# A recommendation tower with held tables: tables and ids laid side by side in memory, fewer and larger loads, and the weights' low halves computed one unit later

## The reference

```python
e = jnp.stack([tbl_0[ids[:, 0]], ..., tbl_25[ids[:, 25]]], axis=1)      # (2048, 26, 128)
combined = jnp.concatenate([e, r_dense_x[:, None, :]], axis=1)          # (2048, 27, 128)
z = jnp.einsum('bfd,bgd->bfg', combined, combined)[:, TRIU_I, TRIU_J]   # (2048, 351)
h = jnp.concatenate([z, r_dense_x], axis=1)
h = jnp.maximum(h @ W_top1 + b_top1, 0.0)      # W_top1 (479, 512)
h = jnp.maximum(h @ W_top2 + b_top2, 0.0)      # W_top2 (512, 256)
y = h @ W_top3                                 # W_top3 (256, 1)
```

## Time and profile before

| | before |
|---|---|
| median of 3 runs | 418.01 (416.83 to 420.61) |
| the profiled execution's own time | 419.08 |
| its span, first to last instruction | 417.0 |
| mean granted TensorE clock in the span | 0.935 |
| busy: PE, PEld, DVE, ACT, POOL | 341.8, 324.6, 248.9, 203.5, 253.0 |
| moved by DMA | 44.80 MB, mean 107 GB/s |

### The profile page before, as it was taken

How to read it: one execution, slowest core, us unless ns; L and a number is a source line. 1 busy time by engine, 2 the same in 40 slices (tenths; PEclk the granted TensorE clock), 3 DMA queues, 4 the chain that set the end, 5 groups by cost and what they waited for, 6 DMA issues and landing times.

```text
span 417.0 us, 9831 instructions
## 1 busy us (share of the span) xinstructions
PE 341.8 (82%) x4178; PEld 324.6 (78%) x4178; DVE 248.9 (60%) x298; ACT 203.5 (49%) x273; POOL 253.0 (61%) x262
## 2 busy tenths in 40 slices
PE   0567679699995999699986999499994999599837
PEld 0566569598995989698986989399994989599736
DVE  3699488744675548754776558564585448662113
ACT  0565584346651385337553474336661475335612
POOL 4788877777777777777777577753777277000000
PEclk9999999889996999999996999889996999979959
DMA  6999525562446325762538225660446315500120
GB/s 175 249 243 255 139 71 149 121 127 52 129 108 132 92 60 150 128 124 53 143 94 138 73 67 149 113 125 23 114 119 123 81 47 146 68 5 2 38 75 0
DMA packets 38237, 44.80 MB, mean 107 GB/s; under 512 B 19561, under 2 KB 31473, under 8 KB 38194
## 3 DMA queue, kind: packets, MB, share of 16 engines
q1 hardware_dynamic: 28602, 24.32, 27.7%
q0 software_dynamic: 8192, 16.79, 16.5%
q10 hardware_dynamic: 1400, 3.07, 2.5%
HBM read 37.95 MB, written 6.20 MB: 106 GB/s over the span
## 4 chain that ended last, share of the span: by engine, by line
PE 50%; DVE 16%; DMA 13%; SPq 7%; issue 7%; ACT 4%; ACTq 3%; DVEq 0%
DVE hot L653 13%; PE ps_gram L434 13%; PE ps_mix L452 11%; PE ps_feat L416 7%; DMA ids_row<-in_ids_t 7%; PE ps_feat L417 7%; DMA products_dram<-gram 6%; SPq L302 6%; PE ps_feat L402 5%; PE ps_mix L485 3%; ACTq L289 2%; SPq L296 2%; PE ps_mix L490 1%; PE ps_feat L452 1%; ACT feat L564 1%
## 5 line engine op out<-in xcount | busy, mean ns | idle before, releaser
L378 POOL DMA_INDIRECT emb<-in_tbl,idx x256 | 252.4, 986 | 100.2 <-issue 76.2
L653 DVE TENSOR_TENSOR hot<-ids_row,ps_rows 125x1024 fp32r<-125x1024 int32 x160 | 186.6, 1215 | 59.6 <-DMA ids_row<-in_ids_t 30.4
L416 PE MATMUL ps_feat<-hot,held_h 125*128 125x256 f32 x640 | 166.4, 297 | 23.9 <-DVE held_l L639 20.1
L564 ACT COPY feat<-ps_feat 128x512 f32<-128x512 f32 x104 | 125.8, 1214 | 76.7 <-PE ps_feat L402 42.8
L417 PE MATMUL ps_feat<-hot,held_l 125*128 125x256 f32 x640 | 161.2, 289 | 0.0
L416 PEld LDWEIGHTS ps_feat<-hot,held_h 125*128 125x128 f32 x640 | 126.8, 198 | 25.9 <-issue 15.2
L417 PEld LDWEIGHTS ps_feat<-hot,held_l 125*128 125x128 f32 x640 | 126.5, 198 | 0.0
L434 PEld LDWEIGHTS ps_gram<-feat 128*54 128x54 f32 x2048 | 54.7, 130 | 11.2 <-ACT feat L564 5.7
L434 PE MATMUL ps_gram<-feat 128*54 128x54 f32 x2048 | 59.8, 215 | 2.5 <-ACT feat L564 2.3
L452 PE MATMUL ps_mix<-z_h,w1z_h 117*128 117x256 f32 x87 | 28.5, 327 | 34.6 <-DVE z_l L695 34.6
L585 ACT ACTIVATE h_h<-ps_mix,b_sb 128x256 fp32r<-128x256 f32 x29 | 13.8, 475 | 86.9 <-DVE h_x L701 86.9
(11 more groups left out here) (77 smaller groups left out, 248.3 us busy)
## 6 DMA issues: line engine op xcount, KB each, us to landing
ids_row<-in_ids_t SPq DMA_DIRECT2D x80, 128.0 KB, 7.1
products_dram<-gram SPq DMA_DIRECT2D x30, 189.0 KB
emb<-in_tbl,idx POOLq DMA_INDIRECT x256
z_raw<-products_dram SPq DMA_DIRECT2D x93, 26.0 KB
held_raw<-in_tbl ACTq DMA_DIRECT2D x5, 448.0 KB
held_raw<-in_tbl SPq DMA_DIRECT2D x5, 448.0 KB
dense<-in_dense_t SPq DMA_DIRECT2D x8, 128.0 KB
w1z_raw<-in_W_top SPq DMA_DIRECT2D x3, 234.0 KB
```

The source lines that it names most:

```text
L378: pool.indirect_dma_start(emb[:, h, f, :], None, table, bass.IndirectOffsetOnAxis(ap=idx[:, i * UNIT + h, f:f + 1].bitcast(u32), axis=0),) ...
L416: nc.tensor.matmul(dst, held_h[:, o, c, :], hot[:, n % 2, c, :], start=c == 0, stop=False)
L564: nc.scalar.copy(feat_v[:, f, b], src).then_inc(act_out, 1)
L653: nc.vector.tensor_tensor(hot[:, n % 2, chunks, :], bass.AP(ids_row, (n % SLOTS) * UC, [[SLOTS * UC, HR], [0, PC], [1, UC]]), row_nums[:, ...
```

## The change

- **Ids.** The ids of the held tables are laid out by unit in one array `ids_h`, one unit's ten tables side by side. One transfer now brings the ids of two tables (`PER_ROW = 2`). There are ten slots, so five transfers a unit, each into its own place; each waits only until the one-hots of the same two tables of the unit before have been made. SP issues all five ahead of the products' store.
- **Held tables.** They are padded to 1024 rows and laid side by side in one array `held` of 128 partitions, so a table is one transfer. ACT issues the ids of the gathers and tables 0 and 1; SP issues the other eight between the id transfers. ACT makes a copy of one element ahead of its first cast. In unit 0 ACT casts three tables ahead, and DVE takes a table's low half before its one-hot, not behind.
- **Weights.** `weights_low` moves from unit 0's product part to unit 1's table part, one behind each one-hot of tables 2 to 7. PE waits for all six at its first l1 step and no longer between units 0 and 1.
- **Smaller.** `store_y` is issued ahead of `products_through_dram`. `h2` shares memory with `z_h`, `y` with `h1_x`, with a wait of ACT and one of DVE for that. The matrix products and one-hots are 128 partitions high and no longer 125.

```diff
-    SLOTS = 7
+    SLOTS = NH
+    PER_ROW = 2
+    AHEAD = 2
...
         def load_table(eng, o):
-            rows_of = held[o][1].rearrange("(p c) d -> p c d", p=HR)
-            for p, end in ((0, EVEN), (EVEN, HR)):
-                eng.dma_start(held_raw[p:end, o, :, :], rows_of[p:end, :, :]).then_inc(held_in[o], 16)
+            eng.dma_start(held_raw[:, o, :, :], held[:, o * HC * D:(o + 1) * HC * D].rearrange("p (c d) -> p c d", c=HC)
+                          ).then_inc(held_in[o], 16)
...
-            def load_ids_row(i, o):
-                n = i * NH + o
-                reached(sp, hot_made, (n - SLOTS + 1) * PIECES)
...
+            def load_ids_rows(i, p):
+                reached(sp, hot_made, ((i - 1) * NH + (p + 1) * PER_ROW) * PIECES)
+                sp.dma_start(ids_row[:, p * PER_ROW:(p + 1) * PER_ROW, :].rearrange("q o b -> q (o b)"),
+                             ids_h[i:i + 1, p * PER_ROW * UC:(p + 1) * PER_ROW * UC].to_broadcast([128, PER_ROW * UC])
+                             ).then_inc(ids_row_in[p], 16)
...
-            sp.dma_start(idx[:], ids_g[:, :, :]).then_inc(ids_in, 16)
-            for o in range(SLOTS):
-                load_ids_row(0, o)
+            load_ids_rows(0, 0)
+            for o in range(AHEAD, NH):
+                if o % PER_ROW == 0:
+                    load_ids_rows(0, o // PER_ROW)
+                load_table(sp, o)
             load_dense(0)
-            for o in range(NH // 2, NH):
-                load_table(sp, o)
-            for o in range(SLOTS, NH):
-                load_ids_row(0, o)
             for i in range(UNITS):
                 if i == 0:
                     weights()
                 if not is_last(i):
-                    for o in range(SLOTS):
-                        load_ids_row(i + 1, o)
+                    for p in range(NH // PER_ROW):
+                        load_ids_rows(i + 1, p)
                     load_dense(i + 1)
-                products_through_dram(i)
-                if not is_last(i):
-                    for o in range(SLOTS, NH):
-                        load_ids_row(i + 1, o)
                 if i > 0:
                     store_y(i - 1)
+                products_through_dram(i)
...
                     if k == 0:
                         pe.wait_ge(dense_low, j + 1)
+                        pe.wait_ge(w_split, NW)
...
-            for o in range(NH // 2):
+            act.dma_start(idx[:], ids_g[:, :, :]).then_inc(ids_in, 16)
+            for o in range(AHEAD):
                 load_table(act, o)
-            for o in range(2):
+            act.wait_ge(cleared, 2)
+            nc.scalar.copy(h1_x[:, 1, 0:1], ones[:])
+            for o in range(3):
                 table_high(o)
...
                     if kind == "hot":
+                        if i == 0 and k[1] == 0:
+                            table_low(k[0])
                         one_hot(i, *k)
-                        if i == 0 and k[1] == PIECES - 1:
-                            table_low(k[0])
+                        if i == 1 and k[1] == PIECES - 1 and k[0] - 2 < NW:
+                            weights_low(k[0] - 2)
...
-                        if i == 0 and k < NW // 2:
-                            weights_low(2 * k)
-                            weights_low(2 * k + 1)
```

More of the change, by code:

```diff
@@ L27, in pairs, with dlrm_tower_kernel @@
     return out
-def dlrm_tower_kernel(nc, x_t, ids_g, ids_t, gathered, held, w1, b1, w2, b2, w3, out):
+def dlrm_tower_kernel(nc, x_t, ids_g, ids_h, gathered, held, w1, b1, w2, b2, w3, out):
     fp32 = mybir.dt.float32
@@ L38, in dlrm_tower_kernel @@
     UC = x_t.shape[1]
-    B, D = ids_t.shape[1], held[0][1].shape[1]
-    NG, NH = len(gathered), len(held)
+    UNITS, NH = ids_h.shape[0], ids_h.shape[1] // UC
+    D = gathered[0].shape[1]
+    B = UNITS * UC
+    NG = len(gathered)
     F = NG + 1 + NH
@@ L44, in dlrm_tower_kernel @@
     UNIT = UC // TILE
-    UNITS = B // UC
     S = 4
@@ L63, in dlrm_tower_kernel @@
     N1, N2 = H1 // 128, H2 // 128
-    ROWS = held[0][1].shape[0]
-    HC = -(-ROWS // 128)
-    HR = ROWS // HC
-    EVEN = HR // 16 * 16
+    HR = held.shape[0]
+    HC = held.shape[1] // (NH * D)
     PIECES = 2
     PC = HC // PIECES
-    SLOTS = 7
+    SLOTS = NH
+    PER_ROW = 2
+    AHEAD = 2
     BANKS = [(f, min(4, NG - f)) for f in range(0, NG, 4)]
@@ L77, in dlrm_tower_kernel @@
     assert UNIT == 2 and N1 == 4 and N2 == 2 and NH % 2 == 0
-    assert ZC * ZR == PAIRS and HC * HR == ROWS and PC * PIECES == HC and GB * M <= BANK
+    assert ZC * ZR == PAIRS and HR == 128 and PC * PIECES == HC and NH % PER_ROW == 0 and GB * M <= BANK
     def merged(*spans):
@@ L140, in dlrm_tower_kernel @@
         h1_x = sb("h1_x", [128, 2, UC], fp32)
-        h2 = sb("h2", [128, N2, UC], fp32)
+        h2 = nc.alloc_sbuf_tensor_at("h2", [128, N2, UC], fp32, offset=placed_at["z_h"])
+        y = nc.alloc_sbuf_tensor_at("y", [1, UC], fp32, offset=placed_at["h1_x"])
         def raw_and_low(name, shape, raw_shape=None, raw_name=None):
@@ L193, in dlrm_tower_kernel @@
         rows_in = [[sem(f"rows_in{h}_{w}") for w in range(NB)] for h in range(UNIT)]
-        ids_row_in = [sem(f"ids_row_in{p}") for p in range(SLOTS)]
+        ids_row_in = [sem(f"ids_row_in{p}") for p in range(NH // PER_ROW)]
         dense_in = sem("dense_in")
@@ L376, in gather @@
                         for f in range(first, first + count):
-                            table = gathered[f][1]
+                            table = gathered[f]
                             pool.indirect_dma_start(
@@ L543, in table_high @@
             def table_high(o):
-                act.wait_ge(held_in[o], 32)
+                act.wait_ge(held_in[o], 16)
                 nc.scalar.copy(held_h[:, o, :, :], held_raw[:, o, :, :]).then_inc(held_high, 1)
@@ L581, in later @@
                     reached(act, l1_done, j * N1)
+                    reached(act, weighed, j)
                     nc.scalar.copy(z_h[:, k, :], z_raw[:, k, :]).then_inc(z_high, 1)
@@ L607, in unit @@
                         later(i - 1, kind, k)
-                    elif kind == "hot" and k[1] == 0 and i == 0:
-                        table_high(k[0])
-            for o in range(NH // 2):
+                    elif kind == "hot" and k[1] == 0 and i == 0 and k[0] + 1 < NH:
+                        table_high(k[0] + 1)
+            act.dma_start(idx[:], ids_g[:, :, :]).then_inc(ids_in, 16)
+            for o in range(AHEAD):
                 load_table(act, o)
-            for o in range(2):
+            act.wait_ge(cleared, 2)
+            nc.scalar.copy(h1_x[:, 1, 0:1], ones[:])
+            for o in range(3):
                 table_high(o)
@@ L698, in later @@
                     dve.wait_ge(l1_done, j * N1 + k + 1)
+                    if k == 0:
+                        reached(dve, y_out, 16 * j)
                     if k >= 2:
@@ L779 @@
     lay["W_top1"] = lay["W_top1"][order]
-    lay["ids_t"] = lay["ids"].T
+    lay["ids_h"] = lay["ids"][:, held].reshape(-1, SAMPLES, HELD).transpose(0, 2, 1).reshape(-1, HELD * SAMPLES)
+    short = -fewest % 128
+    lay["held"] = _np.concatenate([_np.pad(lay.pop(f"tbl_{t}"), ((0, short), (0, 0))).reshape(128, -1) for t in held], 1)
     lay["ids"] = lay["ids"][:, gathered].reshape(-1, 128, len(gathered)).transpose(1, 0, 2)
@@ L792 @@
         ap[name] = nc.dram_tensor(f"in_{name}", a.shape, _mybir.dt.from_np(a.dtype), kind="ExternalInput").ap()
-    rows = lay["ids_t"].shape[1]
+    rows = lay["ids_h"].shape[0] * SAMPLES
     out = nc.dram_tensor("out_y", (1, rows), _mybir.dt.float32, kind="ExternalOutput").ap()
-    dlrm_tower_kernel(nc, ap["dense_t"], ap["ids"], ap["ids_t"], [(t, ap[f"tbl_{t}"]) for t in gathered],
-                      [(t, ap[f"tbl_{t}"]) for t in held], ap["W_top1"], ap["b_top1"], ap["W_top2"],
+    dlrm_tower_kernel(nc, ap["dense_t"], ap["ids"], ap["ids_h"], [ap[f"tbl_{t}"] for t in gathered],
+                      ap["held"], ap["W_top1"], ap["b_top1"], ap["W_top2"],
                       ap["b_top2"], ap["W_top3"], out)
```

10 lines of the change are left out of this document (1 added, 9 removed).

## The result

| | before | after |
|---|---|---|
| median | 418.75 (4 runs, 416.83 to 420.61) | 381.69 (4 runs, 378.92 to 382.68) |
| the profiled execution's span | 417.0 | 379.9 |
| mean granted TensorE clock | 0.935 | 0.978 |
| busy: PE, DVE, ACT, POOL | 341.8, 248.9, 203.5, 253.0 | 333.2, 247.8, 203.5, 252.2 |

The ratio of the times is 0.9105, with a 95% interval of 0.9039 to 0.917. The changed kernel is 37 faster. No engine has much less work: the time was waiting, and matrix work at a low clock.

What follows compares the result with a forecast made beforehand. Late ids held up DVE's one-hots and `z_l`, so PE waited and its clock fell. Terms -1.4 + 3.6 - 3.0 - 23.8 - 11.3 = -35.9, from the median 418.01: 382.1; range 375 to 395, the forecast's own 378 to 387.

Steps and rivals of the forecast that it cites:

- What bounds: Every unit: DVE's one-hots wait for table 7's late ids, so `z_l` is late and PE waits, then runs slowly.
- Ids, units 2 to 7: -23.8: DVE's one-hots in units 2 to 7 no longer wait for ids, as these come ahead of the products: -23.8.
- Clock: -11.3: Units 2 to 7, first z product to l1 chunk 1: PE's clock stays at its upper level, -11.3.
- the rival that it falls all the same: PE's clock behind z falls despite the shorter gap: +11.3, so 393.4; chance 0.16.
- Unit 1: +0.6: Unit 1: weights' low halves among DVE's one-hots cost 3.6, the ids' wait saves 3.0; together +0.6.
- I leave unit 1 its low clock: Unit 1: PE's gap before z stays long, so no clock gain is counted; if the clock stays up, another -2.5.
- The +3.6 and the -3.0: Unit 1: six weights' low halves on DVE add 3.6; the wait for ids that goes saves 3.0.
- Unit 0: -1.4: Unit 0: ACT copies rows 7 earlier, 57.31 to about 55.9, -1.4; bounds 0 and -4.
- at the same time as before: Unit 0: the gathers start when their ids are there, no later than before, and decide the product part's end.
- ACT's lateness: Unit 0: ACT copied rows 7 at 57.31, though PE was done at 55.80; casts of weights lay ahead.
- The gathers: Units 1 to 7: POOL's gathers don't bind, 16 to spare; rival that they bind late units, 388, chance 0.08.
- The low halves and POOL: Unit 1: six weights' low halves cost POOL at most 2.7, hidden in a margin of 9 less 1.7; term 0.

Runs made afterwards that it cites:

- e1: Kernel before with ten id slots, all ids issued ahead of the products' store, and the shared memory of `h2` and `y`; transfers keep 128 KB: 386.19, ratio 0.9202.
- The filler: Kernel before with 28 extra matrix products on PE ahead of its wait for z in units 1 to 7: 405.55, ratio 0.9673.
- e5: Changed kernel with the six low halves of the weights back in unit 0's product part: 376.27, ratio 0.8971.
- e9: Changed kernel with one extra one-hot on DVE, a delay, ahead of table 7's in each of units 2 to 7: 395.77, ratio 0.9437.
- e7: Changed kernel with the gathers' ids in two transfers, unit 0's on ACT's queue, the rest on SP's behind the tables: 380.39, ratio 0.9075.
- e10: Changed kernel with two extra one-hots on DVE, as delays, ahead of table 7's in each of units 2 to 7: 408.72, ratio 0.9747.
- e14: Kernel before with only the ids laid out by unit; seven slots, 128 KB transfers and three late ones as before: 411.52, ratio 0.9834.
- e12: As e1, but the ids come from an array of the ten held tables alone, in long rows by table: 385.81, ratio 0.9192.
- e11: As e1, but the ids come from an array with a unit's ten rows side by side: 377.62, ratio 0.8990.
- e4: Kernel before with the changed kernel's start and `ids_h`; weights' low halves stay in unit 0, ids in seven slots behind the products: 412.65, ratio 0.9823.

## Why the prediction was right, and where it was not

The two large terms and what decides them were right. That the total came within 0.4 of the measured median is luck in part: on the spans the sum of the terms was 1.2 short of the 37.1 measured, with unit 1 better than forecast by 2.6, units 2 to 7 by 0.8, and unit 0 worse by 2.25.

**What bounds.** Right. With the ids ahead of the products and, but for the shared memory, nothing else (e1), units 1 to 7 fall to 41.4 each.

**Ids, units 2 to 7: -23.8.** Right. The units lost 35.9, of which the stretches took 11.5 (next point); the rest is 24.4. PE's six gaps ahead of z shrank by as much, from 30.5 to 6.1.

**Clock: -11.3.** Right: the six stretches fell from 38.63 - 6.03 = 32.60 to 21.09, that is -11.5. I gave the rival that it falls all the same 0.16. The filler and the delays show what decides: PE's gap. But the margin is thinner than I thought. The gap is 1.02, and at 2.27 the clock falls in every unit.

**Unit 1: +0.6, measured -2.0.** The step that failed is the sentence "I leave unit 1 its low clock". The +3.6 and the -3.0 were right, as e5 confirms; the clock stayed up. I had put PE's gap there at 1.1 and up to 1.2 more, and it came out as that, at 2.34:

```profile
82.48 0.35 PE L446 MATMUL ps_mix<-den_h,w1d_h 128*128 128x256 f32 x1 [2.34 <-DVE w_l L642]
```

Behind this same gap of 2.34 the clock stayed up in the changed kernel and in e9, and fell in e7 and e10. So the size of the term, -2.5, was right and given as the other bound; which way it goes here is near chance, as far as one traced execution of each can tell.

**Unit 0: -1.4, measured +0.85.** The +0.85 is less than unit 0 differs by between executions, so whether it became longer is open. But two steps of the term failed. The gathers did not start "at the same time as before": their ids landed later on ACT's queue, and the first gather ran at 6.71 and not at 5.00. The first gather before and after:

```profile
5.00 1.09 POOL L378 DMA_INDIRECT emb<-in_tbl,idx  x1 [3.54 <-DMA idx<-in_ids]
```

```profile
6.71 1.09 POOL L372 DMA_INDIRECT emb<-in_tbl,idx  x1 [5.25 <-DMA idx<-in_ids]
```

In the runs whose whole ids of the gathers are on SP's queue it ran at 4.63 to 5.11, in those that have them on ACT's at 5.47 to 7.01. The second step matters more. The timeline of PE in unit 0, for the earlier trace rows:

```profile
50.68 0.63 PE L396 MATMUL ps_feat<-ident,emb 128*128 128x128 f32 x4 [1.78 <-DMA emb<-in_tbl,idx]
51.24 1.01 PE L428 MATMUL ps_gram<-feat 128*54 128x54 f32 x32
55.34 1.09 PE L396 MATMUL ps_feat<-ident,emb 128*128 128x128 f32 x4 [3.09 <-DMA emb<-in_tbl,idx]
56.36 6.46 PE L428 MATMUL ps_gram<-feat 128*54 128x54 f32 x160
```

```profile
56.36:62.82 6.46, 6.46 (x162) 6.40 (x161) 2.88 (x3) 3.80 (x6) 4.86 (x6) 0.62 0.27 74
```

ACT's lateness did go: it copied rows 7 at 56.46 and not at 57.31. But the table part ended 3.5 earlier, while the 32nd gather, at 52.69 (52.44 before), did not come earlier. PE now waited 1.78 and 3.09 for gathers, and the clock fell to 0.62 in the mean behind that. I applied the rule "a long wait of PE lowers the clock" to the place where the wait went, and not to the place where a new wait came. The two waits, and the low clock behind the second, are in every traced run with the new start. Where the clock stayed up in unit 0 (e14), the last 128 inner products took 3.44 and it ended at 59.13.

**The gathers.** That they don't bind units 1 to 7 was right, with either layout of the ids: all waits for them are in unit 0, and with the old layout the later units are as short (e1: 41.35 and 248.46). What the prediction has no term for is the layout. It took the new one as no more than a means to make one transfer of two. With the ids ahead and the old layout, unit 0 ends 7 later (70.41 and 70.15 against 63.24), with a gather 9.2 late in e1, and 8 to 9 of the gain are gone in the medians (e1 and e12 against e11). The sum came out because the change has both parts. The larger transfers did not show a gain: 80 transfers of 128 KB on the old start (377.62) stand beside 40 of 256 KB on the new one with the low halves in the same place (376.27). The Trainium skill (DMA: Bandwidth & Descriptors, Rules for kernel authors) advises to coalesce many small transfers into one. The run by unit against the one by table (3.4 and 10.1 to landing, at the same size and number) shows that here the place of the rows counted for more.

**The low halves and POOL.** The six in unit 1 cost POOL nothing that PE felt, as forecast; PE had no wait for gathers there.

## What to carry to other kernels

A short wait of a full TensorE costs itself, a slightly longer one also the clock of the work behind it: here 1.25 of delay cost 2.8. So when a change moves waits, list every place where TensorE will newly wait, also those that were hidden before. And before enlarging or merging small transfers, look at which rows they read one after another: the same count and bytes took 34 more of the DMA engines' time from rows 8 KB apart than from rows side by side. Work moved out of a part in which its engine idles, as the low halves were, is a loss unless something there needs the room.

## What the hardware showed that I had not expected

- Repeating a 1 KB row of DRAM on 128 partitions depended on where the next transfer's row lies: 3.4 against 10.1 from issue to landing (medians of 80), and the queue's share 25.0% against 33.3%. It showed without a burst of ten as well: in e14 the landing was 3.8 and the share 22.8%, against 7.1 and 27.7% in the kernel before. The cause is open.
- The clock is not decided by the length of one gap alone. It fell behind one gap of 2.23, six of 2.27 to 2.28, all of 3.38 to 6.18 before the change, and all of 3.14 to 4.76 in e14 and e4. Behind 2.34 it fell twice and stayed twice, and in unit 0 of e14 it stayed up behind this one:

```profile
53.55 0.63 PE L401 MATMUL ps_feat<-ident,emb 128*128 128x128 f32 x4 [2.47 <-DMA emb<-in_tbl,idx]
54.11 1.01 PE L433 MATMUL ps_gram<-feat 128*54 128x54 f32 x32
```

  Ahead of z it never fell behind 1.5 and less. But in unit 0 of e11, where PE had been less busy (2.73 of the 4.00 from 50 to 54), it was 0.52 from 57.14 to 63.23, with no gap over 1.50 ahead. What else goes into it was not separated.
- A gather that falls on a `table_low` of DVE ended 0.81 behind it, at whatever point of it the gather began. So the gathers fall into step with DVE, and a start 0.65 earlier was gone 31 gathers later.
